# A decoder on one Trainium2 core: the recurrent layer's features with its products issued further ahead, the next batch's transposes and mixing inside the current batch, and loads waited for in groups

## The reference

```python
x_last = concat([zeros, x[:, :-1]], axis=1)
dx = x_last - x
mix = tanh((x + dx * x_miu) @ x_A).reshape(B, T, 6, 32)
miu = lambdas + einsum('btgk,gkc->gbtc', mix, x_B)
r_in, w_in, k_in, v_in, a_in, g_in = x[None] + dx[None] * miu
v = v_in @ vW.T
r = r_in @ rW.T
g = tanh(g_in @ g_A) @ g_B
w = -softplus(-(w_miu + tanh(w_in @ w_A) @ w_B)) - 0.5
k = k_in @ kW.T + tanh(k_in @ k_A) @ k_B
k = k / max(norm(k), 1e-12)
a_gate = sigmoid(a_time + a_in @ a_A @ a_B) * 2.0
kk = k * exp(min(w * 0.5, 0.0))
# then wkv7(r, w, kk, v, -k, k * a_gate), and a bonus (r * k * x_time).sum(head) * v
```

## Time and profile before

| | us |
|---|---|
| median of 3 runs (4040.7 to 4043.15) | 4042.92 |
| the profiled execution, its own time | 4046.38 |
| its span in the trace | 4044.2 |
| busy over the span: PE, DVE, ACT, POOL | 3131.8, 2936.5, 1889.8, 1887.6 |
| features (start to the last VectorE instruction of `rwkv_features`) | 0 to 353.3 |

### The profile page before, as it was taken

How to read it: one execution, slowest core, us unless ns; L and a number is a source line. 1 busy time by engine, 2 the same in 40 slices (tenths; PEclk the granted TensorE clock), 3 DMA queues, 4 the chain that set the end, 5 groups by cost and what they waited for, 6 DMA issues and landing times. The chain is left out here.

```text
span 4044.2 us, 46980 instructions
## 1 busy us (share of the span) xinstructions
PE 3131.8 (77%) x16262; PEld 1748.3 (43%) x16262; DVE 2936.5 (73%) x3879; ACT 1889.8 (47%) x2907; POOL 1887.6 (47%) x965
## 2 busy tenths in 40 slices
PE   6775888886562994789988889988889988865833
PEld 2324777775332673234433434434334334333412
DVE  2444566566561113499999999999999999997688
ACT  1323323322240110567766677766677766633434
POOL 0000111112123003187888888888888888871200
PEclk8776777777785997899999999999999999997966
DMA  1000000000003242344443444443444443431000
GB/s 40 0 0 6 1 0 0 0 0 5 19 0 108 84 150 48 112 145 140 158 150 132 147 144 153 149 143 133 149 158 138 146 144 129 149 128 34 1 20 21
DMA packets 120563, 342.19 MB, mean 85 GB/s; under 512 B 14715, under 2 KB 45650, under 8 KB 119666
## 3 DMA queue, kind: packets, MB, share of 16 engines
q1 hardware_dynamic: 114546, 332.01, 24.1%
q0 software_dynamic: 3072, 6.00, 0.7%
q10 hardware_dynamic: 2816, 2.62, 0.2%
HBM read 328.31 MB, written 14.68 MB: 85 GB/s over the span
## 5 line engine op out<-in xcount | busy, mean ns | idle before, releaser
L1913 POOL TENSOR_TENSOR mb_h<-mb_h,mb_BC 128x1024 f32<-128x1024 f32 x512 | 1212.5, 2388 | 404.2 <-DVE mb_h L2160 404.1
L2160 DVE TENSOR_TENSOR_SCAN mb_h<-mb_dA,mb_bx 128x1024 f32<-128x1024 f32 x512 | 1170.4, 2286 | 22.3 <-ACT mb_dA L2027 4.6
L2263 PE MATMUL mb_y<-mb_h,ident 128*128 128x512 f32 x2048 | 1000.7, 628 | 214.0 <-POOL mb_h L1913 212.1
L2027 ACT ACTIVATE mb_dA<-mb_delta,mb_A 128x511 f32<-128x511 f32 x1024 | 664.8, 713 | 416.1 <-DVE mb_h L2160 410.9
L2263 PEld LDWEIGHTS mb_y<-mb_h,ident 128*128 128x128 f32 x2048 | 388.5, 198 | 789.8 <-issue 417.2
L2156 DVE TENSOR_TENSOR mb_bx<-mb_du,mb_BC 128x1024 f32<-128x1024 f32 x512 | 630.2, 1231 | 41.8 <-DMA mb_BC<-mamba_BC 5.4
L254 PE MATMUL mb_p<-mb_xT,mb_in_w 128*128 128x512 f32 x512 | 236.6, 606 | 22.5 <-ACT mb_sz L1953 16.5
L254 PE MATMUL mb_p<-mb_upad,mb_convd 128*128 128x512 f32 x512 | 225.0, 592 | 0.8 <-ACT mb_upad L1941 0.8
L707 POOL COPY rs_vs<-rw_v 128x256 f32 x16 | 9.8, 613 | 444.8 <-PE rs_p L969 336.9
L1637 DVE TENSOR_TENSOR me_h<-me_s,me_p 128x320 f32<-128x320 f32 x64 | 31.2, 487 | 243.0 <-ACT me_s L1614 243.0
L846 DVE TENSOR_TENSOR rs_PQX<-rs_p,rs_PQX 128x128 f32<-128x128 f32 x320 | 85.6, 289 | 113.6 <-PE rs_p L946 112.5
(11 more groups left out here) (441 smaller groups left out, 5697.7 us busy)
## 6 DMA issues: line engine op xcount, KB each, us to landing
mb_BC<-mamba_BC SPq DMA_DIRECT2D x256, 1024.0 KB, 5.2
me_W<-in_L_ffn_W SPq DMA_DIRECT2D x24, 1024.0 KB, 9.1
mb_in_w<-in_L_attn_in_proj_w SPq DMA_DIRECT2D x4, 1024.0 KB, 8.3
mb_convd<-in_mamba_taps SPq DMA_DIRECT2D x4, 1024.0 KB, 10.2
expert_rows<-me_zero SPq DMA_DIRECT2D x1, 2560.0 KB, 10.1
x<-in_x SPq DMA_DIRECT2D x1, 2048.0 KB, 8.4
me_xe<-expert_rows SPq DMA_DIRECT2D x8, 256.0 KB, 10.7
expert_results<-me_oe ACTq DMA_DIRECT2D x8, 256.0 KB, 7.5
```

The lines of the kernel that those rows point to most:

```text
L1913: tt(hk, hk, buffer(k, it)[:, 1, :, :], ALU.mult).then_inc(*pos(f"hc{k}{part}"))
L2027: i = av(dA[k % 2][:, c, s, 1:], delta[:, it % 2, mc, 1:], ACT.Exp, scale=A[:, MC * layer(it) + mc, n:n + 1])
L2160: nc.vector.tensor_tensor_scan(flat(h[k % NBUF][:, c, :, :]), flat(dA[k % 2][:, c, :, :]), flat(full(bx)), 0.0, ALU.mult, ALU.add).then_in ...
L2263: i = mm(ybank[c][:, :], m.ident[:, :], h[k % NBUF][:, c, s, :], start=False, stop=e == HALF - 1 and s == SU - 1)
```

## The change

`setup` has no block of its own any more: its loads move into the features' block. x comes in four pieces, one semaphore each, and the weights on five semaphores (`mix_in`, `mixed_in`, `rw_in`, `kv_in`, `ag_in`), each waited for right before its first use; ones and head sums have a sixth. The copy of x on POOL goes. All four batches are written out in Python; there is no `Fori`. `rf_xT` and `rf_dx` have two places each; w, k and the gate are written straight to their final arrays (`rw_w`, `rw_kk`, `rw_b`). The gate's Sigmoid becomes a Tanh: 2 sigmoid(z) = 1 + tanh(z/2). The decay has two VectorE instructions for four.

TensorE's order in a batch b becomes: miu2, pr, miu3, pw1, key_norm of b-1, miu4, pw2, pk1, miu5, pk2, pv0, pv1, transposes of b+1, pa1, bonus of b-1, pa2, mix of b+1, pg1, miu0 of b+1, pg2, pg3, miu1 of b+1. The core of the diff:

```diff
-                sp.wait_ge(m.x_in, 16)
-                sp.wait_ge(m.consts_in, m.n_consts)
+                rows(0)
+                sp.dma_start(m.ident[:, :], g["identity"]).then_inc(m.consts_in, 16)
+                sp.dma_start(vec[:, :], g["rwkv_columns"]).then_inc(mix_in, 16)
+                sp.dma_start(xA[:, :, :], chunks("L0_attn_x_A")).then_inc(mix_in, 16)
...
+                rows(1)
...
+                rows(2)
+                rows(3)
-            @block.gpsimd
-            def _(pool):
-                pool.wait_ge(m.x_in, 16)
-                with pool.Fori(0, B) as b:
-                    hold(pool, m, pe.turns(b))
-                    nc.gpsimd.tensor_copy(xs[:, :, :], m.x[:, ds(TPB * b, TPB), :]).then_inc(x_staged, 1)
 ```

VectorE's order:

```diff
+                head(0)
+                for b in range(B):
+                    group(b, 0)
+                    group(b, 1)
+                    if b:
+                        decay(b - 1)
+                    group(b, 2)
+                    group(b, 3)
+                    if b:
+                        normalised_key(b - 1)
+                    group(b, 4)
+                    if b:
+                        key_products(b - 1)
+                    if b < B - 1:
+                        head(b + 1)
+                    if b:
+                        bonus(b - 1)
+                    group(b, 5)
+                decay(B - 1)
+                normalised_key(B - 1)
+                key_products(B - 1)
+                bonus(B - 1)
 # ScalarE, order: decay and key_squares of b-1, r, lw, yw, lk,
 # key_norm of b-1, k, v0, v1, la, gate, mix of b+1, lg, g0, g1
+                def key_norm(b):
+                    a.wait_ge(*dve_t.at("w2", b))
+                    nc.scalar.activation(every(hw), every(hw), ACT.Exp, scale=-0.5).then_inc(*act_t("ekk"))
+                    a.wait_ge(*pe_t.at("nrm", b))
+                    a.wait_ge(*dve_t.at("a", b - 1))
+                    nc.scalar.activation(rn[:, :], bank[3][:, :], ACT.Sqrt).then_inc(*act_t("nrm"))
...
+                    if b == B - 1:
+                        decay(b)
+                        key_squares(b)
                     a.wait_ge(*pe.at("pa2", b))
-                        i = nc.scalar.activation(gate[:, c, :], bank[c][:, :], ACT.Sigmoid, bias=col(ATIME, c))
+                        i = nc.scalar.activation(tok(m.b, b, c), bk(c), ACT.Tanh, bias=a_bias(c), scale=-0.5)
+                    if b < B - 1:
+                        mix(b + 1)
 ```

TensorE's start, and the waits of its two moved pieces:

```diff
+                transposes(0)
+                t.wait_ge(mix_in, 32)
+                mix(0)
+                t.wait_ge(mixed_in, 32)
+                t.wait_ge(*act_h.at("mix", 0))
+                t.wait_ge(*dve_h.at("xT", 0))
+                miu(0, 0)
+                miu(0, 1)
...
+                def transposes(b):
+                    t.wait_ge(m.x_in[b], 16)
+                    if b:
+                        t.wait_ge(*dve.at("t4", b - 1))
+                def mix(b):
+                    t.wait_ge(*dve_h.at("xm", b))
+                    if b:
+                        t.wait_ge(*act.at("la", b - 1))
+                        t.wait_ge(*dve_t.at("bonus", b - 2))
```

More of the change, by code:

```diff
@@ L102, in setup @@
     m.passed = sem("passed")
[L103 to L111, removed]
-            sp.wait_ge(m.x_in, 16)
-            sp.wait_ge(m.consts_in, m.n_consts)
+    m.x_in = [sem(f"x_in{b}") for b in range(B)]
+    m.consts_in, m.sums_in = sem("consts_in"), sem("sums_in")
+    m.n_consts = 16
     return m
@@ L304, in rwkv_features @@
-        zeroed = sem("rf_zeroed")
+        mix_in, mixed_in, rw_in, kv_in, ag_in = (sem(f"rf_{n}_in") for n in ("mix", "mixed", "rw", "kv", "ag"))
+        ready = sem("rf_ready")
         signal = lambda name, steps: Steps(sem(f"rf_{name}"), steps, 2)
-        pe = signal("tensor", "xT mix miur miuw pr pw1 miuk pw2 pk1 miuv pk2 pv0 miua pv1 pa1 miug pa2 pg1 pg2 pg3")
-        dve = signal("vector", "xT dx xm tr xdr tw xdw tk xdk tv xdv ta xda tg xdg")
-        act = signal("scalar", "mix r lw yw lk k v0 v1 la gate lg g0 g1")
@@ L309, in rwkv_features @@
-        pe_t, act_t = signal("tensor_t", "nrm bonus"), signal("scalar_t", "abs e1 e2 ekk sq nrm")
-        dve_t = signal("vector_t", "sp w1 w2 hh nmax rn a gb kk rk bonus")
-        def tok(arr, b, c):
-            return arr[:, ds(TPB * b, TPB), c, :]
+        pe = signal("tensor", "pr pw1 pw2 pk1 pk2 pv0 pv1 pa1 pa2 pg1 pg2 pg3")
+        pe_m = signal("tensor_m", " ".join(f"miu{n}" for n in range(6)))
+        dve = signal("vector", " ".join(f"t{n} x{n}" for n in range(6)))
+        act = signal("scalar", "r lw yw lk k v0 v1 la gate lg g0 g1")
@@ L331, in _ @@
[L331 to L335, removed]
[L337 to L343 removed]
+                xin = g["x"].rearrange("b (t p) d -> p (b t) d", p=P)
@@ L390, in decay @@
[L390 to L394, removed]
+                    tsc(line(m.w, b), every(hw), -MIN_LOG_DECAY, -1.0, ALU.min, ALU.mult).then_inc(*dve_t("w2"))
                 def normalised_key(b):
@@ L516, in _ @@
-                body(0, tail=False)
-                with a.Fori(1, B) as b:
-                    body(b)
-                for piece in (decay, key_squares, key_norm):
-                    piece(B - 1)
+                    nc.scalar.activation(low[:, :], bank[6][:, :], ACT.Tanh).then_inc(*act("lg"))
+                    for h in range(2):
+                        a.wait_ge(*pe.at(f"pg{2 + h}", b))
+                        nc.scalar.activation(m.g[:, TPB * b + 2 * h:TPB * b + 2 * h + 2, :], bank[h][:, :].rearrange("p (t n) -> p t n", t=2), ACT.Copy).then_inc(*act(f"g{h}"))
@@ L597, in body @@
[L597 to L602 removed]
+                    t.wait_ge(*dve.at("x3", b))
+                    t.wait_ge(*act.at("k", b))
+                    vpairs = lambda q: [(xd[:, 1, c, chunk(q)], wT["vW"][:, c, :]) for c in range(DC)]
@@ L603, in body @@
+                    token_major("pv0", 0, vpairs)
+                    token_major("pv1", 2, vpairs)
+                    if b < B - 1:
+                        transposes(b + 1)
+                    if b == 0:
+                        t.wait_ge(ag_in, 64)
+                    t.wait_ge(*dve.at("x4", b))
+                    product(nc, bank[2][0:64, :], [(lowA["a"][:, c, :], x_of(4, c)) for c in range(DC)]).then_inc(*pe("pa1"))
+                    if b:
+                        bonus(b - 1)
                     t.wait_ge(*act.at("la", b))
@@ L604, in body @@
                     for mm in range(DC):
-                        i = product(nc, bank[mm][:, :], [(lowB["a"][:, mm * P:(mm + 1) * P], low[0:64, :])])
+                        i = product(nc, bank[mm][:, :], [(lowB["a"][:, chunk(mm)], low[0:64, :])])
                     i.then_inc(*pe("pa2"))
-                    t.wait_ge(*dve.at("xdg", b))
-                    product(nc, bank[2][:, :], [(lowA["g"][:, c, :], x_in(5, c)) for c in range(DC)]).then_inc(*pe("pg1"))
+                    if b < B - 1:
+                        mix(b + 1)
@@ L609, in body @@
+                    t.wait_ge(*dve.at("x5", b))
+                    product(nc, bank[6][:, :], [(lowA["g"][:, c, :], x_of(5, c)) for c in range(DC)]).then_inc(*pe("pg1"))
+                    if b < B - 1:
+                        t.wait_ge(*act_h.at("mix", b + 1))
+                        t.wait_ge(*dve_h.at("xT", b + 1))
+                        miu(b + 1, 0)
+                    gpairs = lambda q: [(low[:, chunk(q)], lowB["g"][:, :])]
                     t.wait_ge(*act.at("lg", b))
-                    gpairs = lambda q: [(low[:, q * P:(q + 1) * P], lowB["g"][:, :])]
```

333 lines of the change are left out of this document (163 added, 170 removed).

## The result

The changed kernel's median is 3926.59 us (3921.58 to 3929.36, 4 runs) against 4043.03 us (4040.7 to 4044.4, 4 runs): ratio 0.9711, 95% interval [0.9694, 0.9728]. It is faster by 116 us, 2.9%; the forecast was 3935.3 (3914 to 3963). The profiled execution took 3921.58 us with a span of 3919.7. It is the fastest of the changed kernel's four runs, and the profiled one of before (4046.38) lay above its median, so the profiled pair differs by 124.8 us where the medians differ by 116.4.

A forecast was written before the change was run, and what follows sets the result against it. TensorE's waits for chains and its low clock were taken to bound the features stage. Start 23.1, batches 44.9 and 2 x 48.1, last batch and tail 60.9, clock 20.6 make 245.7 us, so 3935.3 total (3914 to 3963).

The forecast's parts named there:

- the layout of the steady batch: Looped batches of the features stage, laid out operation by operation at full clock: period 48.1 us against 75.
- the signs named: Trace signs: transposes near 4.5 us, miu2 48 to 54 apart, PE over 90% busy, k wait 1.2, features over near 246.
- The change issues them apart, one more group than now: TensorE's miu products in each batch: formerly side by side, now apart, costing 1.9 us more a batch.
- today's low clock: TensorE in a batch before the change: of 57.3 us busy, about 10.5 was put down to low clock.
- The clock's term: Low clock in the new batches: 4.4 us a batch, 17.6, plus 3 for batch 0's cold start; 20.6 in all.
- The sum at full clock: Whole features stage with TensorE always at full rate, from start through last batch and tail: 225.1 us.
- The clock stays full: Rival: TensorE, kept busy, stays at full rate in the features stage; 225.1 us there, 3914.7 total; chance 0.16.
- The chain sets the period: Rival: in the batches half of today's waiting on the other engines' chain stays, 31 us more, 3966 total; chance 0.14.
- Only start and tail gain: Rival: the loop's chain is merely shifted, so only start and tail save, 15.5 + 12.6 us; 4015 total; chance 0.03.
- Half clock throughout: Rival: TensorE runs all batches at half rate, features 386 us, slower than before at 4076 total; chance 0.03.

The follow-up runs named there:

- e4: Changed kernel with miu2 moved behind r and miu3 behind w's first product, so no two 32-row products are neighbours except in batch 0: 3927.81 us.
- e1: The changed kernel run again, unedited, as the base for the follow-up runs: 3929.56 us, features end at 230.92.
- e3: Changed kernel with mixing products issued in pairs 0+1, 2+3, 4+5 on different rows of the array: 3915.72 us.
- e5: Changed kernel with the next batch's transposes, head, mix, miu0 and miu1 put back behind pg3 on all three engines: 3979.49 us.
- e7: Changed kernel with only the previous batch's Exp, Sqrt, reciprocal and a moved back ahead of group 2: 3965.39 us.
- e6: Changed kernel with miu2 to miu5 put back in their old places (behind pw1, pk1, between pv0 and pv1, behind pa1): 3936.91 us.

## Why the prediction was right, and where not

**Direction and place: right.** TensorE's waits and low clock bounded the stage, and removing them gave the gain. The first transposes came at 4.47 (4.5 taken), the first tanh ended at 19.3 (19.2). The wait for the k copy is 1.27 (1.2), the mix follows pa2 with no wait for xm, and t4 (`rf_tmp` of group 4), for which the transposes wait, is in time: the layout of the steady batch holds operation by operation. PE is busy 97% of batch 2. The tail behind pg3 is 16.2 (16.6). Of the signs named, two did not come: two of the three batches are 45.7 and 45.8 us long, not 48 to 54, and the features are over at 228, not near 246.

**"The change issues them apart, one more group than now" was wrong.** I read the text for one batch and missed that miu1 of a batch ends next to the next one's miu2; in batch 0, miu0 and miu1 stay neighbours as well. There is no more group than before: 48.1 was to be 46.2, and 45.76 was measured. e4 prices the pair at 1.9 a batch. The same slip made today's low clock too small: the 46.8 taken from 57.3 held that extra group. Batch 2 of before has PE busy for 57.1 us and the same batch after, at full clock, for 44.5, so the low clock cost 12.6 a batch, not 10.5.

**The clock's term, 20.6, was too large.** I placed two falls in every batch, in the runs miu1 with miu2 and miu4 with pw2. The first run is one pair of half the length, and no fall came there. The second showed none in the four batches of the first profile; in e1 it did in batch 1, where pw2 took 2.32 and pk1 3.24 for 1.98 and 1.93. The stretches at half clock sum to 9.61 + 3.20 + 6.70 + 2.98 in the rows above, and some more in the last batch's g products: about 24 us of work, so about 12 lost. Of these batch 0 has 4.7, where I took 3, and the other three together 7.3, where 4.4 a batch was 17.6 in all. Falls came at the start, behind the k copy's wait, and around pa2, and vary between runs (the stage ended at 227.85 and 230.92).

The features were forecast at 245.7 and ended at 227.85, 17.9 earlier. The sum at full clock, 225.1, holds 7.6 us for pairs that cost nothing (four of 1.9), and lacks the 12 of low clock: that makes 229.5. The last 1.6 is spread over the layout; the norm product of the tail, taken at 3.78, took 2.84. The total came nearer, 3926.6 for 3935.3, but not by the mechanism: the forecast was tied to the profiled execution of before, and for the profiled pair it was 17.2 off (3938.8 for 3921.58).

**Rivals.** "The clock stays full" is nearer in the features (225.1 for 227.85), the forecast in the median (8.7 off for 11.9). Neither is what happened: the clock did fall, for 12 us and not 20.6, and the rival's sum is near only because the pairs counted twice stand in for most of that. The Trainium skill's rule ("TensorE: Matmul & The Clock Gate", What's actually happening) stands better here than I gave it: over 88.5 us of nearly unbroken work the rate was full. The 6.70 us of unbroken work at 0.50, and the fall behind 6.80 us of it at 1.00, show again that it does not hold of every stretch. "The chain sets the period" is refuted by e3: less TensorE work shortened the batch. "Only start and tail gain" is refuted by the 97.1 us. Half clock throughout: 0.93 was measured.

**What is ascribed to what.** Undone singly on the changed kernel, the parts cost, by the medians and by the features' end: next head inside, 50 and 58; key chain late, 36 and 42; start, 9 and 13; miu products ahead, 7 and 14; last decay inside, 4 and 2. They sum to 107 by the medians, of 116, and to 129 by the features' ends, of 122 from before to e1. They need not sum to the whole, since each wait brings low clock for its neighbours too: put alone on the old kernel, the key chain is worth 20, not 36. No run took back the copy on POOL (before, the transposes wait 1.54 us a batch for it; in e5 they follow with no wait), the unrolled loop, the Tanh for the Sigmoid, or the shorter decay. Open stays why medians move by some us with the same edits, part of it in stages that nobody edited.

## What to carry to other kernels

When an engine's waits come with a lower clock behind them, price a removed wait at more than its length: here a wait of 8.1 us was worth 12 to 14 a batch (e7), and three waits of 6.7 together 17 to 19 (e5), by the medians and the features' ends. Look first for a long chain on a helper engine (Sqrt, reciprocal) that stands in program order ahead of something the main engine needs soon; moving it behind was worth three to five times as much as issuing the products further ahead (e7 against e6). Then use the main engine's own shape: neighbouring small products on different rows of the array share their time.

## What was not expected of the hardware

A term of 1.9 us a batch, plain in the trace, cannot be seen in the median (e4): one program's batches take 45.8, 50.8 or 52.4 us by the clock alone (batches 1 and 2 of the changed kernel and of e1). And eight records of two 32-row products on different rows of the array take 1.99 us, as four alone take 1.98, even where they belong to different steps with a semaphore between them (166.75 us in the profile after).
